# Four reorderings and a deferred sum in a single-core AdaLN block with linear attention and a routed feed-forward

## What is computed

```python
mod = (silu(c) @ wmod).reshape(1, 6, 1, -1)       # sa, ca, ga, sb, cb, gb
h = layernorm(x) * (1 + ca) + sa
# linear attention, K = 2 key/value sets, 16 heads of 16
q  = h + h @ Wq.T + bq ;  ks = h + h @ Wk[i].T + bk[i] ;  vs = h + h @ Wv[i].T + bv[i]
q, ks = unit(silu(q) + 0.5), unit(silu(ks) + 0.5)
state = prod over i of (ks_i^T vs_i)               # per head, 16 x 16
x = x + ga * (layernorm(q @ state) * ln_g + ln_b) @ Wo.T + ...
h = layernorm(x) * (1 + cb) + sb
# feed-forward: 8 experts, the best 2 of each token, and a shared one
scores = sigmoid(h @ gate_w + bias); w = top-2 of scores, normalised
routed = sum over e of w[t, e] * 0.1 * (gelu(h @ up_w[e] + up_b[e]) @ down_w[e] + down_b[e])
shared = (gelu(h @ sw_up + sb_up) @ sw_down + sb_down) * 0.1
x = x + gb * normalise_by_max(shared + routed)
```

## Time and profile before

| | |
|---|---|
| time, median of 3 runs | 953.24 us (952.03 to 953.36) |
| the profiled execution's own time | 950.85 us |
| its span, first to last instruction | 949.0 us |
| mean granted TensorE clock | 0.958 |
| busy share of the span | TensorE 91%, VectorE 67%, ScalarE 50%, GpSimd 42% |

### The profile page before, as it was taken

How to read it: one execution, slowest core, us unless ns; L and a number is a source line. 1 busy time by engine, 2 the same in 40 slices (tenths; PEclk the granted TensorE clock), 3 DMA queues, 4 the chain that set the end, 5 groups by cost and what they waited for, 6 DMA issues and landing times. The chain is left out here.

```text
span 949.0 us, 21404 instructions
## 1 busy us (share of the span) xinstructions
PE 864.0 (91%) x5989; PEld 791.5 (83%) x5990; DVE 635.4 (67%) x1675; ACT 474.6 (50%) x880; POOL 403.0 (42%) x415
## 2 busy tenths in 40 slices
PE   6999999999889789899879999989999999999980
PEld 5778878888778678688669999989999999999980
DVE  5789885659778568578756665566565566666652
ACT  3766553253543434435357655565554455555530
POOL 3633500303243151342600656554565565655564
PEclk9999999789999999999979999999999999999995
DMA  8120000822142141230662333352343343344442
GB/s 283 63 89 1 1 1 1 269 48 55 60 114 46 70 115 22 92 90 25 214 215 67 84 93 86 84 178 54 87 89 84 87 90 91 80 80 78 93 83 48
DMA packets 68609, 83.31 MB, mean 88 GB/s; under 512 B 23088, under 2 KB 56842, under 8 KB 68400
## 3 DMA queue, kind: packets, MB, share of 16 engines
q0 software_dynamic: 25792, 39.92, 18.0%
q1 hardware_dynamic: 41392, 41.12, 13.8%
q10 hardware_dynamic: 1344, 1.31, 0.4%
HBM read 45.44 MB, written 41.55 MB: 92 GB/s over the span
## 5 line engine op out<-in xcount | busy, mean ns | idle before, releaser
L1849 PE MATMUL psUp<-eT,wup 128*128 128x256 f32 x1632 | 208.6, 289 | 10.4 <-issue 8.8
L1849 PEld LDWEIGHTS psUp<-eT,wup 128*128 128x128 f32 x1632 | 202.3, 195 | 15.6 <-issue 14.5
L1871 PE MATMUL psE<-wdn,gTh 128*128 128x256 f32 x1088 | 200.4, 286 | 0.0
L1871 PEld LDWEIGHTS psE<-wdn,gTh 128*128 128x128 f32 x1088 | 169.5, 192 | 0.0
L1871 PE MATMUL psE<-wdn,gTl 128*128 128x256 f32 x544 | 154.0, 283 | 0.0
L1929 ACT ACTIVATE ys<-yc,meta 128x256 f32<-128x256 f32 x68 | 30.9, 502 | 181.9 <-DVE yc L1996 150.5
L2113 POOL DMA_INDIRECT out<-fin,oidx x68 | 109.1, 1604 | 22.8 <-issue 16.8
L1910 ACT ACTIVATE gu<-psUp,ubias 128x256 f32<-128x256 f32 x272 | 113.4, 468 | 7.6 <-PE psUp L1849 4.7
L1975 DVE TENSOR_TENSOR gTl<-gu,gTh 128x512 fp32r<-128x512 f32 x136 | 93.8, 690 | 32.4 <-ACT gTh L1915 24.5
L2103 POOL DMA_INDIRECT shared_part<-ys,widx x68 | 70.8, 1042 | 97.6 <-ACT ys L1929 53.7
L1160 PE MATMUL psU<-h2T,su 128*128 128x512 f32 x384 | 103.9, 409 | 8.8 <-ACT gf L1254 7.8
(11 more groups left out here) (296 smaller groups left out, 1448.6 us busy)
## 6 DMA issues: line engine op xcount, KB each, us to landing
hin<-expert_in SPq DMA_DIRECT2D x36, 256.0 KB
X<-in_L_attn_x SPq DMA_DIRECT2D x8, 512.0 KB, 7.5
X<-bo_row POOLq DMA_DIRECT2D x8, 512.0 KB
shared_part<-prow SPq DMA_DIRECT2D x8, 512.0 KB, 6.0
out<-X SPq DMA_DIRECT2D x8, 512.0 KB
shared_part<-sh SPq DMA_DIRECT2D x7, 512.0 KB
raw_up<-in_L_ffn_up_w SPq DMA_DIRECT2D x3, 1024.0 KB
raw_dn<-in_L_ffn_down_w SPq DMA_DIRECT2D x3, 1024.0 KB, 10.6
```

The source lines that it names most:

```text
L1849: mm = nc.tensor.matmul(psU[:, c, (m % 2) * TR:(m % 2 + 1) * TR], wup[s][:, a, k, m * P:(m + 1) * P], eT[:, u, b, k], start=(n == 0), stop ...
L1871: mm = nc.tensor.matmul(psE[:, u, h * C:(h + 1) * C], (gTh, gTl)[a][:, u, m, h * P:(h + 1) * P], wdn[s][:, b, m], start=(n == 0), stop=(n ...
```

## The change

It has six parts, with no change to what is computed:

1. Stage 1, ScalarE: in group 1 `scale_values` and `project` stand behind the two `query` calls, not ahead of them.
2. Stage 1, start: TensorE does the key bias ahead of the first transposes, VectorE adds it ahead of `low(0, ...)`.
3. Stage 2, last body, TensorE: `rank()` stands ahead of `up(2)` rather than behind it.
4. Stage 2, last body: the two halves of the up weights' high part stand behind `gelu(5)` and `gelu(6)` on ScalarE; on VectorE the first low half stands between `table_used` and `low_g(6)`, the second at the end as before.
5. The last `shared_read` is moved over the barrier to VectorE's start of stage 3, `psY` is kept for that and doubles as stage 3's `psE`; its store is issued by SyncE there, between the first `meta` load and that of `dbias`; the first `down` waits for the read.
6. Stage 3, first tile: `turn_h(1)` stands in the middle of `up(0)` (behind chunk 1 of 4), and `high` and `low` of tile 1 one chunk sooner.

```diff
@@ stage 1, ScalarE, group g
-                if g == 1:
-                    scale_values()
-                    project()
                 if g < LATER:
                     query(g, 0)
                 if g == 0:
                     output()
                 if g < LATER:
                     query(g, 1)
+                if g == 1:
+                    scale_values()
+                    project()
@@ stage 1, TensorE
-            turn(0, 0)
-            turn(0, 1)
...
             mm.then_inc(kb_mm, 1)
+            turn(0, 0)
+            turn(0, 1)
@@ stage 1, VectorE
+            dve.wait_ge(ld_b, 32)
+            dve.wait_ge(kb_mm, 1)
+            nc.vector.tensor_tensor(bk_row[:], psR[:, 1], bk_row[:], ALU.add).then_inc(kb_ok, 1)
             low(0, 0)
             low(0, 1)
             statistics(1)
-            dve.wait_ge(ld_b, 32)
-            dve.wait_ge(kb_mm, 1)
-            nc.vector.tensor_tensor(bk_row[:], psR[:, 1], bk_row[:], ALU.add).then_inc(kb_ok, 1)
@@ stage 2, TensorE
                 chunk(1)
+                if not att_on:
+                    rank()
...
-                if att_on:
-                    chunk(2)
-                else:
-                    up(2)
-                    rank()
-                    down(0)
+                chunk(2)
@@ stage 2, ScalarE, last body
                     for m in range(MK):
                         gelu(m)
-                    split_hi(act, 0, 0, (0,))
+                        if m in (5, 6):
+                            split_hi(act, 0, 0, (0,), (m - 5,))
...
-            act.wait_ge(sh_ev, 2 * NG)
-            act.dma_start(shd_v[:, TG * (NG - 1):NT, :], sh[:]).then_inc(sh_st, 16)
@@ stage 2, VectorE, last body
                     table_used()
+                    split_lo(dve, 0, 0, (0,), (0,))
                     low_g(6)
                     table_slots()
                     low_g(7)
                     table_next()
-                    split_lo(dve, 0, 0, (0,))
-                    shared_read(f)
+                    split_lo(dve, 0, 0, (0,), (1,))
@@ stage 3
-        psE = mem.enter_context(nc.psum_tensor("psE", [P, 2, HALF], F32))
+        psE = psY
@@ stage 3, SyncE
             load_tails(sp, entry(sp, rtab, 0, E * REG - TR), 0)
+            sp.wait_ge(sh_ev, 2 * NG)
+            sp.dma_start(shd_v[:, TG * (NG - 1):NT, :], sh[:]).then_inc(sh_st, 16)
             sp.dma_start(dbias[:], down_b.partition_broadcast(P)).then_inc(db_in, 16)
@@ stage 3, TensorE
-            up(0, 0)
-            turn_h(1, 1, 0)
+            up(0, 0, lambda: turn_h(1, 1, 0))
@@ stage 3, ScalarE
-            chunks(0, 0, entry(act, etab, 0, E - 1))
+            chunks(0, 0, entry(act, etab, 0, E - 1), 2)
@@ stage 3, VectorE
+            dve.wait_ge(d_mm, MK * NG)
+            dve.wait_ge(sh_st, 16 * (NG - 1))
+            for h in range(2):
+                nc.vector.scalar_tensor_tensor(sh[:, 2 * h:2 * h + 2], psE[:, h].rearrange("p (t c) -> p t c", c=C), 0.1,
+                                               sbd_row[:].unsqueeze(1).broadcast_to([P, 2, C]), ALU.mult, ALU.add
+                                               ).then_inc(sh_ev, 1)
             low(0, 0)
             split_lo(dve, 0, 0, (1,))
             for c in range(MC):
-                if c == MC - 1:
+                if c == 2:
                     low(1, 1)
```

More of the change, by code:

```diff
@@ L994, in weights, with split_hi @@
         sp.dma_start(raw_dn[:], down_v[bass.ds(e, 1)].rearrange("a p k n -> p (a k) n")).then_inc(dn_in, 16)
-    def split_hi(act, n, s, which=(0, 1)):
+    def split_hi(act, n, s, which=(0, 1), halves=(0, 1)):
         for i in which:
@@ L1001, in split_hi, with split_lo @@
             dst = (wup, wdn)[i][s][:, 0].rearrange("p k n -> p (k n)")
-            for h in range(2):
+            for h in halves:
                 at = slice(h * W // 2, (h + 1) * W // 2)
                 nc.scalar.copy(dst[:, at], src[:, at]).then_inc(w_hi, 1)
-    def split_lo(dve, n, s, which=(0, 1)):
+    def split_lo(dve, n, s, which=(0, 1), halves=(0, 1)):
         for i in which:
@@ L1014, in split_lo @@
                 ins = nc.vector.tensor_tensor(lo[:, at], src[:, at], f32(hi[:, at]), ALU.subtract)
-            ins.then_inc(w_ok, 1)
+            if halves[-1] == 1:
+                ins.then_inc(w_ok, 1)
     names = ("o_mm", "o_ev", "stat2", "self2", "rse2",
@@ L1036, in adaln_block @@
     PASSES = ((0, 0), (0, 1), (1, 0))
+    psY = ctx.enter_context(nc.psum_tensor("psY", [P, 2, HALF], F32))
     with ExitStack() as mem, nc.Block() as block:
         psU = mem.enter_context(nc.psum_tensor("psU", [P, 2, HALF], F32))
-        psY = mem.enter_context(nc.psum_tensor("psY", [P, 2, HALF], F32))
         psZ = mem.enter_context(nc.psum_tensor("psZ", [P, 2, HALF], F32))
@@ L1829, in turn_h, with up @@
                 mm.then_inc(ht_mm, 1)
-            def up(j, u):
+            def up(j, u, between=None):
                 slot = entry(pe, stab, j, 2)
@@ L1853, in up @@
                             mm.then_inc(eu_mm, 1)
+                            if between is not None and c == 1:
+                                between()
             def down(j, u, more, i):
@@ L1865, in down @@
                             pe.wait_ge(ey_ev, j - 1)
+                        elif j == 0:
+                            pe.wait_ge(sh_ev, 2 * NG)
                         pe.wait_ge(eu_lo, MC * j + MC)
@@ L1915, in chunk, with chunks @@
                 nc.scalar.copy(gTh[:, u, 2 * c:2 * c + 2], gu[:, c % 2]).then_inc(eu_hi, 1)
-            def chunks(j, u, e):
+            def chunks(j, u, e, turn=MC - 1):
                 for c in range(MC):
-                    if c == MC - 1:
+                    if c == turn:
                         high(j + 1, 1 - u)
```

## The result

| | before | changed |
|---|---|---|
| time of this measurement, median of 5 | 952.03 us (945.99 to 953.36) | 942.85 us (939.66 to 946.46) |
| the profiled execution, its span | 950.85, 949.0 us | 939.66, 937.8 us |
| mean granted TensorE clock | 0.958 | 0.976 |

The ratio on record is 0.9925, with a 95% interval from 0.9904 to 0.9946: about 7.1 us won, between 5.1 and 9.1. (The two medians of five alone differ by 9.2 us; executions of one kernel lie several us apart, so the ratio with its interval is used from here on.) The prediction had the direction and, with 5.5 us, a gain inside that interval, but its time of 947.7 and its range from 945.8 both lie above the measured 942.85.

A forecast was written before the change was run, and what follows sets the result against it. TensorE, busy 91% of the span, was taken as the bound, with gains only where it idles. Terms 0.5 + 0 + 4.6 + 0.4 = 5.5 us, against the median 953.24, gave 947.7 us; range 945.8 to 950.9.

The forecast's parts named there:

- The level: Whole kernel: the gain was set against the median of the runs shown, 953.24 us, giving 947.7.
- The clock: Half clock behind stage 2's gap and at stage 3's start may fall elsewhere: up to 1 us either way per case.
- projection later: Stage 1, second query: TensorE's 1.74 us wait goes, most returns ahead of group 3's transposes; 0.5 us won, 0 to 1.74.
- key bias: Start of stage 1: four products moved into TensorE's idle time for `xn`; 0 us, at worst 0.2 later.
- ranks sooner, at the boundary: Stage 2's last body: `place` starts 1.19 us sooner (0 to 1.19), raising the barrier's gain from 2.8 to 4.6 us.
- halves and sums, at the boundary: Last barrier: 1.18 us for a half and 1.28 for the sums leave VectorE's end, ScalarE's 0.4 issue goes; 2.8 us.
- second tile's transposes: Stage 3, second `up`: the 1.45 us wait goes, part returns as a wait for tile 2's rows; 0.4 us won.
- start of stage 3 at a higher clock: Start of stage 3: 48 matmuls took 8.55 us, later 5.99; clock shifts allowed up to 1 us either way.
- rival A: Stage 2's last body: the ranks' signal stays late, so only 3.7 us are won, 949.5 us; chance 0.22.
- So only 0.5 us is free if these land as before: Stage 3, tile 2's transposes: loads in flight ended about 504.4 against transposes at 504.94, limiting the 1.45 us gain.
- rival B: Start of stage 3: the shared sums' store delays the loads by 1.4 us, a 0.9 loss, 949.0 us; chance 0.16.
- The Trainium skill's rule: SyncE's store ahead of stage 3's row loads: completions land after earlier writes, putting the second tile's term at 0 or below.

The follow-up runs named there:

- e14: The changed kernel repeated unchanged on the first chip, against the kernel before: ratio 0.9923 (0.9892 to 0.9953).
- e18: The changed kernel repeated unchanged on the fourth chip, paired with the kernel before: ratio 0.9912 (0.9883 to 0.9941).
- e17: The kernel before, unchanged, run again for a trace on the fourth chip: ratio 0.9995 (0.9973 to 1.0018).
- e2: The kernel before with only the second tile's transposes moved into the first tile's `up`: ratio 1.0004 (0.9987 to 1.0021), median 949.18 us.
- e4: The kernel before with only the ranks moved ahead of the third `up`: ratio 1.0007 (0.9989 to 1.0025), median 949.84 us.
- e13: The changed kernel with the ranks put back behind the third `up`, on the first chip: ratio 0.9923 (0.9898 to 0.9948).
- e15: The changed kernel without sooner key bias and ranks, with unread filler matmuls around the barrier of stages 1 and 2: ratio 0.9930 (0.9902 to 0.9957).
- e1: The kernel before with only the split halves and the shared sums moved over the barrier: ratio 0.9956 (0.9937 to 0.9975), median 945.34 us.
- e8: The changed kernel with six unread matmuls filling TensorE's gap behind stage 2's last `down`: ratio 0.9947 (0.9924 to 0.9970).
- e12_after: The changed kernel repeated unchanged on the third chip, against the kernel before: ratio 0.9958 (0.9940 to 0.9976).
- e5_after: The changed kernel repeated unchanged on the second chip, against the kernel before: ratio 0.9920 (0.9889 to 0.9951).
- e6: The changed kernel with SyncE's stage 2 stores of `out` reordered, the last behind the first expert's weight loads: ratio 0.9934 (0.9908 to 0.9959).

## Why the prediction was off

Five measurements of the changed kernel gave 0.9925, 0.9920, 0.9958, 0.9923 and 0.9912. Weighted by their intervals the mean is 0.9934, with an interval of about 0.9923 to 0.9945 if they measured one thing: 6.3 us of 950. The third chip's value fits the other four badly (their mean is 0.9921).

The measured 942.85 is 4.9 us below the forecast of 947.7. Two thirds of that are the level from which the gain was taken off, the rest is the size of the gain.

**The level: the step that failed first.** "The median of the runs shown is 953.24, 2.4 above it; against that, 947.7." That median was of three executions. The same measurement had 952.03 in five, and on chips with like times the kernel before has 948.87, 950.18 and 950.06 in 74 executions. With 950 in place of 953.24 the same 5.5 us give 944.5. The profile's own 950.85 would have been the better anchor, and gave 945.3; both are still above 942.85. The changed kernel's 942.85 itself is no outlier: it had 943.65 and 942.35 in e14 and e18.

**The clock: the second.** "I give this up to 1 us either way inside each case." Granted clock moves by more than that in code that nobody touched: the kernel before had 0.74 from 160 to 200 us in one trace, the same stretch 0.83 in e17, and 0.87 and 0.74 in two traces of the changed kernel (e18, e14). Over the 35 executions of before on the first chip the mean granted clock goes from 0.958 to 0.974, and the time falls by about 0.37 us for each 0.001 (0.16 to 0.50 in the other four sets). The range of 5 us that I gave was made of the rivals' sizes alone, and is narrower than the 8 us over which executions of one kernel scatter.

**The terms**, in the order of the sum:

| term | predicted | in the traces |
|---|---|---|
| projection later | 0.5 (0 to 1.74) | 0.46 |
| key bias | 0, at worst 0.2 later | not to be told from 0 |
| ranks sooner, at the boundary | 1.8 of the 4.6 | 0.1 to 0.3 |
| halves and sums, at the boundary | 2.8 | 3.0 (1.28 and 1.71) |
| second tile's transposes | 0.4 (up to 1.45) | 1.6 |
| start of stage 3 at a higher clock | up to 1 either way | about 0.5 |

The first four are read at their place, the fifth from e2 against e4. The last is what is left of the 5.3 us: 5.3 - 3.0 - 0.2 - 1.6 = 0.5. Its largest piece is visible: the first transposes, 1.08 us long in the earlier trace rows and 0.63 after, let the first `up` start 0.46 us sooner.

The places add up to 5.8 us where 5.5 were predicted. That this fits is luck: the ranks were put 1.6 us too high, and the second tile and the clock together 1.7 too low.

Stage 1: the working held, step by step, with the new wait of 0.52 us on `xn` where it was foreseen. The other new wait, 0.53 us for VectorE's `kn` ahead of the sums, was not.

Ranks: the step "I take 1.19, since the ranks no longer stand behind an `up` whose own end is also in doubt" failed, and rival A was right. In the trace after and in e4 the ranks end 0.7 us sooner, and `place` starts 3.92 and 3.88 us behind `ohb`, against 4.01 before. On the third chip, where the signal is prompt, `place` stood behind VectorE's own `choose_rest`, with part 3 or without. And where `place` did come 0.8 us sooner (e14 and e18 with part 3, 3.2 us behind `ohb`, against e13 and e15 without, 4.0), SyncE's load of `raw_up` was issued only 0.3 us sooner (10.2 against 10.5) and the transposes came 0.3 sooner (26.00 and 26.05 against 26.32).

Halves and sums: the term was right to 0.2 us. 1.18 + 1.28 + 0.4 was predicted in pieces, 1.28 and 1.71 were measured.

Second tile: the mechanism was right and the size was wrong. The step that failed is "So only 0.5 us is free if these land as before". In the trace before, the last of the sixteen increments by which the load of tile 2's rows reports its landing stands at 504.12 us, so the earlier trace rows was read rightly: they were among the loads that ended late. But that landing is the latest of all twenty traces, and it is not fixed in time. SyncE issues this load 6.5 to 6.9 us behind the first transposes in all twenty traces, so it moves with the boundary. And the last increment comes 18.02 us behind the first transposes in the trace before (the fifteen others by 15.58), 16.24 to 17.60 in the other five without part 6, and 16.21 to 16.90 in the fourteen with it. Why it came so late in that one trace isn't known. The load does bound the gain in the changed kernel, with 0.84 us.

The store ahead of the rows costs nothing that shows, and rival B fell. In the fourteen traces in which SyncE issues it (parts 4 and 5) it goes out 1.4 us behind the first transposes and has landed by 4.6 to 4.8, at least 1.6 us before the load of tile 2's rows is even issued. With it ahead of them, part 6 still shortens the way to tile 2's transposes from 18.31 (e1) to 16.56 us (the trace after). The Trainium skill's rule that I weighed there (DMA: Bandwidth & Descriptors, Queues, rings and completion order) is about earlier writes that are still under way; none of this store's were, so it gave no ground for 0 or below.

Clock at the start of stage 3: e8 shows the cause, since filling the gap brings back the full clock (24 matmuls in 3.10 us against 4.46 to 5.46).

What stays open: 5.3 and 0.46 make 5.8 us, inside the pooled interval (5.2 to 7.3) and inside the first measurement's (5.1 to 9.1). That these places are all of it is argued from traces; e2's ratio doesn't bear out its share of it. On the four measurements outside the third chip 7.5 us were gained, 1.7 more than the places show, and on the third 3.8. Whether the change also makes half-clock stretches rarer, or how it depends on the chip, the runs don't settle.

## What to carry to other kernels

Take the level from the execution whose rows you sum, and ask first how far executions of one kernel scatter; a range can't be narrower than that. Work moved over a barrier is priced well by its own rows, but a wait that is removed in front of a load is worth what the load allows, so find that one transfer's landing against its own issue, and in more than one trace: here it lay 1.8 us apart between traces. TensorE paid twice for its idle time at the barrier, once for the gap and once with the clock behind it; filling the gap gave back the second, and lost it again behind the next wait.

## What the runs showed of the hardware

**Signals of TensorE arrive late on some chips.** (A signal is the increment of a semaphore that a waiting engine needs.) The last ranks in e14_after, on the first chip, TensorE and then VectorE:

```profile
455.16 0.24 PE L1149 MATMUL psM<-ohb,one_b 128*128 128x8 bf16 x4
```

```profile
458.01 0.19 DVE L1459 TENSOR_TENSOR rk<-psM,run 128x32 f32<-128x32 f32 x1 [0.33 <-remote]
```

and in e12_after, the same program on the third chip:

```profile
436.42 0.24 PE L1149 MATMUL psM<-ohb,one_b 128*128 128x8 bf16 x4
```

```profile
438.26 0.18 DVE L1459 TENSOR_TENSOR rk<-psM,run 128x32 f32<-128x32 f32 x1
```

The reader, ready by 457.7, is released 2.6 us behind the ranks' end in the first, and doesn't wait in the second. In the semaphore events of the first trace over 90 of TensorE's signals come more than 0.5 us behind the modelled end of their matmul, and in the earlier groups they are up to 4.7 us late; in e12_after there is none. The traces of the first, second and fourth chip have 85 to 103 such signals each, the four of the third chip none or one. What one can do is seen in e5_after, on the second chip: an `up` ends at 464.19, its signal comes at 466.63, and so 2.4 of the 3.91 us for which ScalarE stands idle are the signal's:

```profile
466.65 0.69 ACT L1252 ACTIVATE gf<-psU,sbu 128x512 f32<-128x512 f32 x1 [3.91 <-remote]
```

Two groups in the middle of stage 2, e14_after first:

```profile
305.00:381.00 76.00, 65.62 (x433) 55.28 (x432) 51.30 (x163) 32.37 (x48) 23.65 (x26) 1.00 0.25 71
```

```profile
301.00:368.00 67.00, 64.33 (x438) 55.60 (x437) 51.39 (x165) 32.48 (x49) 24.26 (x27) 1.00 0.29 81
```

The same work, at the full clock in both, takes 76 us on one chip and 67 on the other. From the first group's `ohb` to the last's it is 242 against 224 us, and from the first transposes of stage 3 to the end 462 against 451. That the late signals are what makes the difference is likely but not shown, and their number alone doesn't set it: the second chip has as many, with 236 and 455 us in e5_after. Near the late ranks SyncE's stores of `out` are in flight; with those moved away (e6) the ranks' signal was late all the same, so what holds the signals back isn't known.
